# Attention's differences and weights read from PSUM, another order of pairs, and the opening of a decoder layer in another order

## What is computed

```python
def _layernorm(x, axis=-1, eps=1e-05):
    m = jnp.mean(x, axis=axis, keepdims=True)
    v = jnp.var(x, axis=axis, keepdims=True)
    return (x - m) / jnp.sqrt(v + eps)

# first attention: x is [T=4, B=512, 256]
q = jnp.einsum('tbm,mhd->tbhd', x, q_weight)
q_sq = jnp.einsum('tbhd,tbhd->tbh', q, q)
squared_dist = q_sq[:, None] + q_sq[None, :] - 2.0 * jnp.einsum('tbhd,sbhd->tsbh', q, q)
attn_weights = jax.nn.softmax(-squared_dist * inv_sqrt_d, axis=1)
A = jnp.einsum('mhd,nhd->hmn', q_weight, q_weight) * inv_sqrt_d
XA = jnp.einsum('tbm,hmn->tbhn', x, A)
PXA = jnp.einsum('tsbh,sbhm->tbhm', attn_weights, XA)
PXAV = jnp.einsum('tbhm,mhd->tbhd', PXA, v_weight).reshape(x.shape[0], x.shape[1], -1)
return PXAV @ out_w.T + out_b
...
x = x + _L0_attn_ref(_layernorm(x), ...)
x = x + _L0_xattn_ref(_layernorm(x), ctx_1024, ctx_1024, ...)
x = x + _L0_ffn_ref(_layernorm(x), ...)
```

## Time and profile before

| what | us |
|---|---|
| median of 3 runs | 424.45 (422.96 to 425.5) |
| the profiled execution's own time | 424.85 |
| its span, first to last instruction | 423.1 |
| part 1, until the first product of part 2 (L805) | 0 to 114.95 |
| mean granted clock of TensorE | 0.904 |

### The profile page before, as it was taken

How to read it: one execution, slowest core, us unless ns; L and a number is a source line. 1 busy time by engine, 2 the same in 40 slices (tenths; PEclk the granted TensorE clock), 3 DMA queues, 4 the chain that set the end, 5 groups by cost and what they waited for, 6 DMA issues and landing times.

```text
span 423.1 us, 6126 instructions
## 1 busy us (share of the span) xinstructions
PE 327.0 (77%) x2169; PEld 290.5 (69%) x2169; DVE 310.0 (73%) x699; ACT 189.3 (45%) x340; POOL 204.2 (48%) x239
## 2 busy tenths in 40 slices
PE   0786968487988899999999973111399999999991
PEld 0674756374666799999999972000299989999991
DVE  3069899996557889888888854887447787789950
ACT  3346465245554464756666454100032565452330
POOL 3706875951111336588887878200214235524622
PEclk9969799979999999999999996555579999999997
DMA  8920000000000003412531535200026577612322
GB/s 261 381 82 2 2 0 2 0 0 0 0 2 0 2 12 126 135 56 110 161 102 38 174 121 181 85 1 0 25 57 200 144 224 208 177 20 45 51 26 25
DMA packets 24046, 34.26 MB, mean 81 GB/s; under 512 B 1785, under 2 KB 20561, under 8 KB 23889
## 3 DMA queue, kind: packets, MB, share of 16 engines
q1 hardware_dynamic: 20112, 29.36, 21.2%
q0 software_dynamic: 3072, 4.20, 5.5%
q10 hardware_dynamic: 832, 0.32, 0.4%
HBM read 27.58 MB, written 6.29 MB: 80 GB/s over the span
## 4 chain that ended last, share of the span: by engine, by line
PE 53%; DVE 25%; DMA 7%; POOL 5%; issue 5%; ACT 4%; POOLq 0%; DVEq 0%; ACTq 0%
PE bank L838 13%; PE bank L839 12%; PE bank L840 12%; DMA xg<-xn_rows,idx 6%; DVE flags_all L1171 3%; PE bank L859 3%; PE bank L805 2%; DVE stats L525 2%; PE bank L1289 2%; DVE dist L608 2%; DVE G_lo L537 1%; PE bank L901 1%; PE bank L1319 1%; DVE H_lo L824 1%; DVE acc L567 1%
## 5 line engine op out<-in xcount | busy, mean ns | idle before, releaser
L1379 POOL DMA_INDIRECT xg<-xn_rows,idx x16 | 20.1, 1259 | 85.6 <-DVE idx L1453 83.2
L1349 ACT ACTIVATE hbuf<-bank,b_cols 128x256 f32<-128x256 f32 x64 | 26.9, 472 | 55.5 <-PE bank L840 51.9
L961 POOL TENSOR_TENSOR prob<-prob,rsum 128x1024 f32<-128x1024 f32 x16 | 30.5, 1906 | 21.3 <-DVE rsum L1055 19.8
L838 PE MATMUL bank<-xgT_hi,W_hi 128*128 128x256 f32 x128 | 37.3, 291 | 1.4 <-DVE xgT_lo L1443 1.4
L838 PE MATMUL bank<-H_hi,PT_hi 128*128 128x256 f32 x128 | 36.3, 284 | 1.7 <-DVE PT_lo L1032 1.7
L838 PE MATMUL bank<-W_hi,h_hi 128*128 128x256 f32 x128 | 37.3, 292 | 0.0
L839 PE MATMUL bank<-xgT_lo,W_hi 128*128 128x256 f32 x128 | 37.1, 290 | 0.0
L840 PE MATMUL bank<-xgT_hi,W_lo 128*128 128x256 f32 x128 | 37.0, 289 | 0.0
L840 PE MATMUL bank<-H_hi,PT_lo 128*128 128x256 f32 x128 | 36.2, 283 | 0.0
L839 PE MATMUL bank<-H_lo,PT_hi 128*128 128x256 f32 x128 | 36.2, 283 | 0.0
L840 PE MATMUL bank<-W_hi,h_lo 128*128 128x256 f32 x128 | 36.2, 282 | 0.0
(11 more groups left out here) (230 smaller groups left out, 1028.4 us busy)
## 6 DMA issues: line engine op xcount, KB each, us to landing
W_raw<-in_L_ffn_W SPq DMA_DIRECT2D x16, 1024.0 KB, 5.2
X<-in_x SPq DMA_DIRECT2D x4, 512.0 KB, 9.1
xn_rows<-xn SPq DMA_DIRECT2D x16, 128.0 KB, 1.8
out_x<-X SPq DMA_DIRECT2D x4, 512.0 KB, 3.8
Wq<-in_L_xattn_Wq SPq DMA_DIRECT2D x1, 1024.0 KB, 9.2
Wk<-in_L_xattn_Wk SPq DMA_DIRECT2D x1, 1024.0 KB, 11.8
Wv<-in_L_xattn_Wv SPq DMA_DIRECT2D x1, 1024.0 KB, 15.2
Wo<-in_L_xattn_Wo SPq DMA_DIRECT2D x1, 1024.0 KB, 11.9
```

The source lines that it names most:

```text
L838: t.matmul(out_ps, hi, rhs_hi, start=first, stop=False)
L961: g.tensor_tensor(prob[:, s], prob[:, s], rsum[:, s].unsqueeze(2).to_broadcast([P, HX, CK]), ALU.mult).then_inc(prob_ready, 1)
L1349: ins = a.activation(hbuf[:, g % 2, f % 2], banks[g][:, (f % 2) * CAP:(f % 2 + 1) * CAP], ACT.Gelu_apprx_tanh, bias=b1_cols[:, e * FC + f: ...
L1379: g.indirect_dma_start(xg[:, s, h], None, xn3_dram, bass.IndirectOffsetOnAxis(ap=idx[:, e, h:h + 1], axis=0), bounds_check=ROWS - 1, oob_i ...
```

## The change

1. **Operands in PSUM.** Banks 2 and 3 become one tensor, `q_banks`. One of the two operands of each difference is read from there, the other from the copy in SBUF as before. `ex`, `den` and `rden` move to bank 7. So of each DVE instruction that combines two tensors in a block before `pair_sums`, and of `scale`, one operand lies in PSUM.
2. **Pairs** are ordered (0,1), (0,2), (0,3), (2,3), (1,3), (1,2), so that each difference subtracts an SBUF operand from a PSUM one, and so that a position's three exponentials stand at one step from each other; ex has a seventh row, a copy of the first, which ACT writes with an activation of its own. The denominators are four reduces over three rows each, in place of four additions.
3. **Opening.** SP loads the small weights before the second block of x, and all of x earlier than Wk. PE starts with ctxT, owT and MT, then the first block. All four blocks' statistics come first on DVE; the WqT copies go around the first block's steps. POOL writes only the mask before the second `inverse_std`, the other tables after it, and the third and fourth after these. `normalise(2)`, `xnT_evac(1)` and `q_evac(1)` move to the opening on ACT.
4. **The loop.** G uses banks 5 and 6 alone, since bank 7 holds ex. y goes to banks 0 and 1 (those of the transposes). V is a step of its own, behind the transposes of M on PE. On ACT the copy of the next K and `G_evac` stand before the exponentials. The banks of q are given back by DVE's differences. `low_parts(0)` moves from s = 0 to s = 1, before `scale(0)`.

```diff
-    PAIRS = [(0, 1), (1, 2), (2, 3), (0, 2), (1, 3), (0, 3)]
+    PAIRS = [(0, 1), (0, 2), (0, 3), (2, 3), (1, 3), (1, 2)]
...
+        q_banks = ctx.enter_context(nc.psum_tensor("q_banks", [P, T, D], F32))
+        banks += [q_banks[:, 2 * m:2 * m + 2].rearrange("p a n -> p (a n)") for m in range(2)]
...
+        ex = banks[7][:, 0:(NP + 1) * HS].rearrange("p (a h) -> p a h", h=HS)
+        den = banks[7][:, 128:128 + T * HS].rearrange("p (a h) -> p a h", h=HS)
+        rden = banks[7][:, 256:256 + T * HS].rearrange("p (a h) -> p a h", h=HS)
...
-            return (K_next + [(f"G{c}{m}", 5 + (MC * c + m) % 3, G_ready, MC * c + m + 1) for m in range(MC)]
+            return [(f"G{c}{m}", 5 + m, G_ready, MC * c + m + 1) for m in range(MC)]
...
-            bank, by = {"T": (0, xnT_ready), "M": (0, mixT_ready), "q": (2, q_ready), "y": (2, x1_ready)}[what]
+            bank, by = {"T": (0, xnT_ready), "M": (0, mixT_ready), "q": (2, dif_ready), "y": (0, x1_ready)}[what]
...
             sp.dma_start(wqa[:], wq_s).then_inc(ld["wqa"], 16)
-            load_x(1)
             sp.dma_start(ctx_sb[:], ctx_rows).then_inc(ld["ctx"], 16)
             sp.dma_start(owa[:], ow_s).then_inc(ld["attw"], 16)
             sp.dma_start(wva[:], wv_s).then_inc(ld["attw"], 16)
+            load_x(1)
+            load_x(2)
             sp.dma_start(Wq[:], chunked(A["L0_xattn_Wq"])).then_inc(ld["wq"], 16)
+            load_x(3)
             sp.dma_start(Wk[:], chunked(A["L0_xattn_Wk"])).then_inc(ld["wk"], 16)
-            load_x(2)
-            load_x(3)
...
             inverse_std(slice(1, NT, NJ), var1_ready, 2, rstd1_ready)
+            pool_more_tables(pool, order)
+            for j in range(2, NJ):
+                inverse_std(slice(j, NT, NJ), var1_ready, j + 1, rstd1_ready)
...
-                a.activation(ex[:], dist[:], ACT.Exp, scale=-1.0 / HD ** 0.5).then_inc(ex_ready, 1)
+                a.activation(ex[:, NP], dist[:, 0], ACT.Exp, scale=-1.0 / HD ** 0.5)
+                a.activation(ex[:, 0:NP], dist[:], ACT.Exp, scale=-1.0 / HD ** 0.5).then_inc(ex_ready, 1)
...
+                v.tensor_tensor(w[:, 0:3], q_banks[:, 1:4], Q[:, 0:1].to_broadcast([P, 3, D]), ALU.subtract)
+                v.tensor_tensor(w[:, 3:5], q_banks[:, 3:4].to_broadcast([P, 2, D]), Q[:, 2:0:-1], ALU.subtract)
+                v.tensor_tensor(w[:, 5:6], q_banks[:, 2:3], Q[:, 1:2], ALU.subtract).then_inc(dif_ready, 1)
...
+                for t, first, step in ((0, 0, 1), (1, 4, 1), (2, 1, 2), (3, 2, 1)):
+                    ins = v.tensor_reduce(den[:, t], ex[:, first:first + 2 * step + 1:step].rearrange("p a h -> p h a"),
+                                          AX.X, ALU.add)
```

231 lines of the change are left out of this document (131 added, 100 removed).

## The result

| what | before | after |
|---|---|---|
| median of 5 runs, us | 424.77 (422.96 to 425.5) | 411.04 (408.82 to 411.64) |
| ratio to before, 95% interval | | 0.967 (0.965 to 0.970) |
| the profiled execution's own time | 424.85 | 408.82 |
| its span | 423.1 | 407.0 |
| mean granted clock of TensorE | 0.904 | 0.916 |

The kernel is 13.7 us faster, by the medians. One execution further down, the profiled one of "squares first", is over 1.5% above the fastest of its kernel, counts as slow and is left out of that kernel's ratio. What the traces locate is this 16.0.

The account below looks back on a forecast made before the run. Part 1 was taken as paced by the four weighings, with DVE busiest but partly waiting for POOL. From 424.85, -9.2 - 0.7 - 1.4 - 3.2 = -14.5, tail 0, gave 410.4 us; range 406.5 to 416.

Parts of the forecast that it names:

- Opening: Up to the first weighing: reordered loads, statistics and POOL tables, and no wait for POOL, bring it from 38.08 to 28.9, -9.2 us.
- What PSUM costs: DVE and ACT instructions with bank operands, repeated elements included: taken as no slower than SBUF, 0 us.
- Rival D: Slower: bank operands with a repeated element run much slower on DVE, 421.1 at half rate, 431.7 at a third; chance 0.03 plus 0.02.
- the 2.3 us that would have made 412.7: Larger fixed part for a bank, 120 cycles against 58, on some nine instructions a block: 0.6 us each block, 2.3 in all.
- Round 1: First to second weighing: 16.4 against 17.1, -0.7 us, as DVE idles some 4 us for squares behind ACT's and PE's chain.
- rival A: PE's clock falls after a 2 us idle before the last WqT transposes, slowing q product, K and G: +3 us, 413.4; chance 0.22.
- Rival C: The chain of ACT and PE in round 1 is shorter, the round going down towards 13.6: 407.6; chance 0.12.
- Rounds 2 and 3: Second to fourth weighing: POOL's pair sums set the pace, 14.4 against 15.8 and 14.2 against 17.4, so -1.4 and -3.2 us.
- Tail: Fourth weighing to part 2: G's two banks, V's new place and PE's clock taken as cancelling, 0 us, between -1 and +2.5.
- B: DVE's waits for POOL remain in part despite bank operands, leaving the opening's reordering and perhaps 1 us of the rounds: 416.7; chance 0.08.
- E: The opening's gain is missing because x(1) or Wq land later and PE waits: up to 5 us lost, 415.4; chance 0.11.
- cast beside a pair sum: In round 1 the cast of trials, operands in SBUF, may be held 1.3 us by POOL; DVE's idle time hides it.

Follow-up runs that it names:

- squares first: Changed kernel with block 1's squares on ACT moved ahead of the copy of K and xnT, its exponentials ahead of G_hi: 408.27 us, 0.961 of before.
- Tables first: Changed kernel with POOL's tables back in front of the second block's 1/sqrt: 413.51 us, 0.975 of before.
- WqT earlier: Changed kernel with the second pair of WqT copies on DVE moved ahead of the first block's distances: 407.00 us, 0.962 of before.
- WqT, squares and products: Changed kernel with early second WqT copies, block 1's squares and exponentials earlier on ACT, and four unused PE products in the tail: 407.37 us, 0.963 of before.
- differences and ex from SBUF: Two kernels, each the changed one with one group back in SBUF: the differences' operands, 413.14 us (0.972 of before); ex, den and rden, 414.80 us (0.980).
- order alone: Changed kernel with all operands back in SBUF, its order, new pairs and reduces kept: 415.56 us, 0.980 of before.
- products in the tail: Changed kernel with four extra PE products that nobody reads, filling two waits around chunk 6's K: 410.70 us, 0.971 of before.

## Why the prediction was right

The forecast of 410.4 lies 0.6 us below the median, and the mechanism was the one that it named: with an operand in PSUM DVE no longer waits for POOL, and the opening no longer stands behind POOL's tables. That it is as near as 0.6 is in part luck. The sum was laid out between profiled executions, and there it was 14.5 against 16.0 measured; this execution of after lies 2.2 us below its median. At part 2's first product it was 14.5 against 16.8, since most terms erred to one side and only round 1 to the other.

**Opening, -9.2 forecast, -10.7 measured.** x(1)'s statistics start at 10.19 rather than 10.7, and PE does the first eight transposes in 1.30 us where 1.97 was laid out. The differences begin at 18.09 (19.3 forecast). A part of this is the execution: of ten traces with this order of transfers it has the earliest landing of the small weights, 7.98, where the others have 8.0 to 11.5. The order of steps held: xn(2), from 23.46, is what stands ahead of the exponentials. Tables first gives the tables' part in it by the timings, some 3.3 us.

**What PSUM costs, 0 forecast.** L628 takes 1.74 against 1.76 and L596 1.22 against 1.23, both with a repeated bank operand. Rival D is refuted at its root. The addition of 1 to 64 columns, 0.23 from a bank and 0.20 from SBUF, and 0.02 each for the reciprocal and the change of sign behind it, are all that a bank cost, under 0.1 us a block. Of the 2.3 us that would have made 412.7 there is nothing to see: 512 columns with a bank operand took 0.68 (50.78), as they did before from SBUF where nothing held them (23.21).

**Round 1, -0.7 forecast, +0.7 measured.** The wait of DVE for the squares is 3.86 us, forecast at some 4, and the chain of V's bank, K, its copy and xnT is the right one. What failed is its start and one term of it. The last WqT copies ended not at 25.3 but at 24.03, 1.3 early; then the q product, put in at 3.72, took 5.30. That is rival A's mechanism in its place, at 1.6 rather than 3 us: "PE is busy almost without a break for the 10 us before" overlooked gaps of 1.09 and 2.57 us: DVE makes the first two WqT copies behind its differences and the next two behind its distances. The product ended at 29.9, where the forecast's terms put it at about 29.7. So the second weighing was forecast at 45.35 and came at 45.16, and round 1 is longer only because the first weighing came 1.5 early. WqT earlier confirms the place: some 2 to 3 us gained. Rival C was wrong as a forecast but right as a direction: the shorter chain of WqT, squares and products has a round 1 of 12.3 us, and pays most of it back in round 2.

**Rounds 2 and 3, -1.4 and -3.2 forecast, -2.05 and -3.66 measured.** Pair sums of 1.27 set the pace, with waits of 0.57 and 0.98 us for them, forecast at about 1. The half microsecond too much is spread over small steps: from the exponentials to the weighing 1.6 rather than 1.8, and several instructions on DVE start some 0.1 us before the end of the one in front. The prediction called round 3 the longest before because a den instruction was held as well as the differences. That was so in all three rounds (2.33, 1.08 and 2.38 us of den); the last was only the longest. And the stretch of 32 to 106 us in the earlier trace rows is slices 4 to 10, counted from 1; what was read from it stands.

**Tail, 0 forecast within -1 and +2.5, -1.07 measured.** The profiled execution has the clock at 0.76 from the fourth weighing up to 80 us and at 1.00 from there on; squares first has it at 0.50 for a stretch and a tail 2.7 us longer, differences and ex from SBUF 2.6 and 2.5. Against the 26.5 of before these are +1.7, +1.6 and +1.5, so both sides of the bound were met, and its lower end was just passed.

**Rivals.** B (the waits remain) would have been 416.7, and order alone, where they do remain, takes 415.56. E wasn't met in this execution; in traces with later weights the first weighing came up to 1.6 us later (products in the tail, 28.93), and none of it was left at the second, behind the faster q product. The prediction's cast beside a pair sum was held (1.23 us, at 30.62), at no cost in time, as it said.

**Open.** The profiled execution of after is 2.2 us below its median. The products in the tail brought no gain, which speaks against the tail as the cause but doesn't rule it out. Its early weights, a fast or slow q product behind the gap, and the parts behind part 1, which differ by up to 2.1 us between the traces, could each make it up; no trace of a slower execution of after shows it. What the reduces save by themselves is open, too.

## To carry to other kernels

When DVE and POOL work side by side, look for DVE instructions that end together with POOL's; putting one operand into PSUM, or using a reduce in place of additions, frees them at no cost per column, but the bank stays taken until DVE has read it, so a product that used it needs another one. Then look at PE's gaps: faster DVE work leaves PE waiting, and a gap of 1.7 to 4 us in front of a product can, in some executions and not in others, cost 1.6 to 2.7 us of slow clock on top of the wait, so a step that feeds PE goes ahead of one that only DVE and ACT need.

## What the runs showed of the hardware

- A tensor_scalar of 64 fp32 columns, SBUF to SBUF, beside a POOL addition: 2.09 and 1.41 us, against 0.20; a cast of 60 columns 1.23, against 0.19 before. Reduces beside the same POOL addition: 0.14 each (0.55 for four), not held. Beside POOL's own steps on 4 columns (1.04 us) a reciprocal took 0.55 and a tensor_scalar of 64 columns 0.20, in the kernel before at 87.61 and 87.38: not held either.
- The cost is on both sides: POOL's pair sums of 1.27 took 1.87 and 1.96 beside a DVE instruction with two SBUF operands.
- An operand in a bank, repeated or not, costs what it costs in SBUF: 1.74 for 1536 columns, 1.22 for 1024, and 0.68 for 512.
- The clock after a gap isn't certain: 1.66 us idle was followed by 0.50 (3.75 us for four products of 512 columns), 2.57 us by a q product of 5.30 in one trace and of 3.62 in another of the same instructions, 1.82 us by four products of 3.75 in one trace and of 1.96 in another, 5.74 us in the kernel before by slow transposes (1.91) but a fast y (3.72), 3.97 us by a slow y (6.10).
- In the opening the rows give a clock of 1.00 all the same where PE is slow: eight transposes took 1.30 us in after (10.88) and 1.91 in order alone (11.24), and order alone's first q product took 5.60.
- The same transfers in the same order landed between 7.98 and 11.51 us, by the start of the step that waits for the last of them.
